# Routing the second and third sequence inside the tail of attention

## The reference

```python
x = x + L0_attn(layernorm(x))   # 16 heads of 8, causal, ALiBi bias; out @ Wo + bo
x = x + L0_ffn(layernorm(x))    # 8 experts, top 1, capacity 4096/8 = 512:
#   logits = x @ Wr + br ; gate = max(softmax) ; idx = argmax
#   pos = cumsum(one_hot(idx)) over all tokens in order ; kept where pos < capacity
#   out = gate * (relu((gate*x) @ W1[idx] + b1) @ W2[idx] + b2)
x = x + L1_attn(layernorm(x))   # attention over the 4 sequences at each position, tanh before softmax
x = x + L1_ffn(layernorm(x))    # x @ weight.T + pooled(x) @ disha
```

## Time and profile before

| | us |
|---|---|
| median of 3 runs | 681.1 (679.51 to 681.44) |
| profiled execution, its own time | 678.24 |
| its span, first to last instruction | 676.0 |
| last maximum of attention ends | 474.6 |
| first matmul of the routing stage | 505.24 |
| first load of the experts' rows | 562.12 |
| mean granted TensorE clock | 0.913 of full |

### The profile page before, as it was taken

How to read it: one execution, slowest core, us unless ns; L and a number is a source line. 1 busy time by engine, 2 the same in 40 slices (tenths; PEclk the granted TensorE clock), 3 DMA queues, 4 the chain that set the end, 5 groups by cost and what they waited for, 6 DMA issues and landing times. The chain is left out here.

```text
span 676.0 us, 13740 instructions
## 1 busy us (share of the span) xinstructions
PE 534.4 (79%) x4905; PEld 251.8 (37%) x4905; DVE 501.2 (74%) x1035; ACT 418.7 (62%) x737; POOL 234.8 (35%) x333
## 2 busy tenths in 40 slices
PE   3774798899999899998898888988867617957774
PEld 1441233333233223333333233333127615835563
DVE  4999878889888888789895988889008732626796
ACT  1971278787887787787786767867861412316651
POOL 2563012212212215222323224621621671078821
PEclk9886599999999999999999999989998757976897
DMA  7379355466533353121340120401013247310122
GB/s 181 88 175 280 99 128 119 116 149 196 145 83 68 67 114 67 39 42 31 68 89 19 41 56 28 121 20 37 10 25 114 71 136 284 111 28 21 35 48 63
DMA packets 66891, 61.11 MB, mean 90 GB/s; under 512 B 12121, under 2 KB 56058, under 8 KB 66812
## 3 DMA queue, kind: packets, MB, share of 16 engines
q1 hardware_dynamic: 58100, 53.93, 31.6%
q0 software_dynamic: 2560, 3.38, 1.7%
q10 hardware_dynamic: 6164, 2.94, 1.6%
HBM read 33.03 MB, written 29.85 MB: 93 GB/s over the span
## 5 line engine op out<-in xcount | busy, mean ns | idle before, releaser
L933 DVE TENSOR_REDUCE neg_max<-bank 128x2 f32<-128x1024 f32 (+2 forms) x320 | 341.4, 1113 | 62.8 <-PE bank L829 60.0
L973 ACT ACTIVATE probs<-ring 128x512 f32<-128x512 f32 (+4 forms) x480 | 301.8, 682 | 73.6 <-PE ring L857 62.7
L857 PE MATMUL ring<-q_operand,k_operand 56*128 56x512 bf16 (+3 forms) x768 | 161.7, 331 | 18.7 <-ACT probs L973 13.9
L878 PE MATMUL sums<-probs,v_all 128*9 128x512 f32 (+3 forms) x1536 | 161.5, 493 | 6.6 <-POOL probs L1022 4.3
L1022 POOL TENSOR_SCALAR_AFFINE_SELECT probs<-probs 128x512 f32<-128x512 f32 x128 | 80.5, 634 | 210.8 <-ACT probs L973 210.4
L829 PE MATMUL bank<-k_operand,q_operand 54*128 54x512 bf16 (+3 forms) x768 | 141.4, 340 | 9.1 <-DVE v_all L613 5.3
L857 PEld LDWEIGHTS ring<-q_operand,k_operand 56*128 56x128 bf16 x768 | 49.4, 94 | 146.0 <-ACT probs L973 103.9
L823 PE MATMUL bank<-masks 64*128 64x128 bf16 (+2 forms) x768 | 70.9, 225 | 6.8 <-DVE neg_max L933 5.8
L829 PEld LDWEIGHTS bank<-k_operand,q_operand 54*128 54x128 bf16 x768 | 46.0, 97 | 26.7 <-DVE neg_max L933 15.1
L823 PEld LDWEIGHTS bank<-masks 64*128 64x128 bf16 x768 | 36.2, 96 | 40.9 <-DVE neg_max L933 27.2
L1469 POOL DMA_INDIRECT early<-expert_out,back x32 | 32.7, 1022 | 38.3 <-issue 38.3
(11 more groups left out here) (208 smaller groups left out, 657.5 us busy)
## 6 DMA issues: line engine op xcount, KB each, us to landing
q_operand<-q_rows SPq DMA_DIRECT2D x64, 96.0 KB, 3.8
k_operand<-k_rows SPq DMA_DIRECT2D x32, 192.0 KB, 4.5
q_rows<-early SPq DMA_DIRECT2D x36, 128.0 KB, 2.4
k_rows<-early SPq DMA_DIRECT2D x36, 128.0 KB, 2.4
expert_rows<-fill SPq DMA_DIRECT2D x16, 257.0 KB, 4.2
rows<-expert_rows SPq DMA_DIRECT2D x8, 514.0 KB, 6.6
weighted_sums<-osum SPq DMA_DIRECT2D x126, 18.0 KB
sums_in<-in_L_attn_x SPq DMA_DIRECT2D x4, 512.0 KB, 7.3
```

Source lines behind the costliest of these rows:

```text
L857: last = nc.tensor.matmul(psS[:, bank, w * j:w * j + w], k_op[rows, buf, p, P * kb:P * kb + P], q_op[rows, buf, c, p, q0:q0 + w], start=Tr ...
L878: last = nc.tensor.matmul(psO[32 * i:32 * i + HD + 1, q0:q0 + w], v_all[:, n, kb, i, :], probs[:, u % NPROBS, i // 2, i % 2, 0:w], start=u ...
L933: nc.vector.tensor_reduce(neg_max[:, n % 2, slot, kc, :, pairs[0]:pairs[-1] + 1, t % CH], src, AX.X, ALU.max, negate=True).then_inc(a_read, 1)
L973: nc.scalar.activation(dst, src, ACT.Exp).then_inc(ring_read, 1)
```

## The change

The routing of the second and third sequence (chunks 2 to 5) up to their places moves from the routing stage to the tail of attention, behind the last maximum. The results of the matmuls go to the four halves of the maxima's banks. A new table `TAIL_AT` places the steps by tick (116 is unit 8 of group 14, 131 the last unit of group 15); all of TensorE's stand in the queue right behind the weighted sums of that unit. The copies of columns and the scales are VectorE's here, the power stays with GpSimd, the exponential of the logits with ScalarE. `add_bias` moves from ticks 23 and 24 to 11 and 12 for every sequence. What the routing stage keeps of sequences 1 and 2 is gating (now in steps of one chunk) and the sends.

```diff
-EARLY_AT = {6: ["reciprocals"], 7: ["store_reciprocals"], 9: ["load_reciprocals"], 20: ["divide"], 21: ["divide"],
-            23: ["bias"], 24: ["bias"]}
+EARLY_AT = {6: ["reciprocals"], 7: ["store_reciprocals"], 9: ["load_reciprocals"], 11: ["bias"], 12: ["bias"], 20: ["divide"], 21: ["divide"]}
+TAIL_AT = {116: [("project", 2)], 117: [("project", 3), ("add", 2), ("add", 3), ("moments", 2)],
+           119: [("turned", 2), ("columns", 2), ("moments", 3), ("power", 1)], 120: [("turned", 3), ("columns", 3), ("scales", 1)],
+           121: [("logits", 2)], 122: [("project", 4)], 123: [("logits", 3), ("choose", 1), ("add", 4), ("moments", 4)],
+           124: [("project", 5)], 125: [("counts", 1), ("exps", 1), ("add", 5), ("moments", 5), ("power", 2)],
+           126: [("turned", 4), ("columns", 4), ("place", 1)], 127: [("turned", 5), ("columns", 5), ("scales", 2)],
+           128: [("logits", 4)], 129: [("logits", 5), ("choose", 2)], 131: [("counts", 2), ("exps", 2), ("place", 2)]}
+TAIL_PE = {"project": 900, "turned": 700, "logits": 500, "counts": 500}
+LATE_PROJ, LATE_TURN, LATE_LG = {2: 0, 3: 1, 4: 1, 5: 3}, {2: 2, 3: 3, 4: 0, 5: 1}, {1: 0, 2: 3}
...
+            for name, c in TAIL_AT.get((n - H // GH - 1) * NU + u, []):
+                assert not a_todo
+                order.append(("E", n, "late_" + name, c // QC, c))
+                pe += TAIL_PE[name] + 2 * DRAIN if name in TAIL_PE else 0
...
+                def late_project(k):
+                    if k == QC:
+                        pe.wait_ge(a_read, NG * NM)
+                    elif k == QC + 2:
+                        pe.wait_ge(x1_ready, QC + 2)
+                    elif k == QC + 3:
+                        pe.wait_ge(late_xt, 2)
+                    pe.wait_ge(at_ready, k + 1)
+                    for i in range(CH):
+                        last = nc.tensor.matmul(half[LATE_PROJ[k]][:, P * i:P * i + P],
+                                                ot[:, k // QC, CW * (k % QC) + P * i:CW * (k % QC) + P * i + P], w["wo"][:, :],
+                                                start=True, stop=True)
+                    last.then_inc(late_proj, 1)
+                def late_turned(k):
+                    pe.wait_ge(x1_ready, k + 1)
+                    if k == QC + 2:
+                        pe.wait_ge(lg_ready, 2)
+                    for i in range(CH):
+                        last = nc.tensor.transpose(half[LATE_TURN[k]][:, P * i:P * i + P], rows[:, CH * k + i, X1:X1 + D], ident[:, :])
+                    last.then_inc(late_turn, 1)
+                def late_logits(k):
+                    pe.wait_ge(late_xt, k - QC + 1)
+                    if k == 2 * QC:
+                        pe.wait_ge(x1_ready, 3 * QC)
...
+                def late_counts(b):
+                    pe.wait_ge(hot_ready, b + 1)
+                    pe.wait_ge(late_xt, 1)
+                    pe.wait_ge(slot_ready, b)
+                    place_counts(b, half[2][:, 0:KB * E]).then_inc(late_pos, 1)
...
+                def late_add(k):
+                    dve.wait_ge(late_proj, k - QC + 1)
+                    dve.wait_ge(xb_ready, k + 1)
+                    x1 = rows[:, CH * k:CH * k + CH, X1:X1 + D]
+                    nc.vector.tensor_tensor(x1, x1, half[LATE_PROJ[k]].rearrange("p (i d) -> p i d", i=CH), ALU.add).then_inc(x1_ready, 1)
+                def late_columns(k):
+                    dve.wait_ge(late_turn, k - QC + 1)
+                    if k >= 2 * QC:
+                        dve.wait_ge(late_lg, k - 2 * QC + 1)
+                    nc.vector.tensor_copy(r["xt2"][:, k % 2, :], half[LATE_TURN[k]]).then_inc(late_xt, 1)
...
+                        elif name == "late_power":
+                            pool.wait_ge(ve2_ready, QC * (c + 1))
+                            t = slice(KB * c, KB * c + KB)
+                            nc.gpsimd.tensor_tensor(r["rs2"][:, t], r["ve2"][:, t], half_pow[:, 0:KB], ALU.pow).then_inc(pw2_ready, 1)
...
-        items["gated", r] = ("act", 3800 if r < EARLY else 1900, 0, [("place", r)])
+        for i in range(QC if r < EARLY else 1):
+            items["gated", QC * r + i] = ("act", 1900, 0, [("place", r)])
...
-            items["send", u] = ("pool", 1280, 0, [("gated", r)] if u < TILES - CH else [("gated_last", 0)])
-    for i in [(name, k) for name in ("project", "add", "moments", "turned", "columns", "logits", "take") for k in GROUPS[0]]:
+            items["send", u] = ("pool", 1280, 0, [("gated", u // CH)] if u < TILES - CH else [("gated_last", 0)])
+    for i in [(name, k) for name in ("project", "add", "moments", "turned", "columns", "logits", "take") for k in range(K0)]:
         del items[i]
-    for name in ("power", "scales", "choose", "exps", "counts", "place", "gated"):
-        del items[name, 0]
+    for i in [(name, b) for name in ("power", "scales", "choose", "exps", "counts", "place") for b in range(EARLY)] + [("gated", c) for c in range(QC)]:
+        del items[i]
...
-    K0, K1 = QC * EARLY, QC
+    K0 = K1 = QC * EARLY
```

More of the change, by code:

```diff
@@ L881, in weighted_sums @@
                     last.then_inc(pv_done, 1)
+                def late_project(k):
[22 more added lines that the diff above has]
+                        pe.wait_ge(x1_ready, 3 * QC)
+                    for i in range(CH):
+                        c0 = E * (CH * (k % QC) + i)
+                        last = nc.tensor.matmul(half[LATE_LG[k // QC]][:, c0:c0 + E], r["xt2"][:, k % 2, P * i:P * i + P], wrc[:, :],
+                                                start=True, stop=True)
+                    last.then_inc(late_lg, 1)
+                def late_counts(b):
[3 more added lines that the diff above has]
+                    place_counts(b, half[2][:, 0:KB * E]).then_inc(late_pos, 1)
                 for kind, n, *args in ORDER:
@@ L946, in _ @@
                         maxima(n, *args)
+                    elif kind == "E" and args[0] == "late_add":
+                        late_add(args[2])
+                    elif kind == "E" and args[0] == "late_moments":
+                        dve.wait_ge(x1_ready, args[2] + 1)
+                        router.moments(dve, args[2])
+                    elif kind == "E" and args[0] == "late_columns":
+                        late_columns(args[2])
+                    elif kind == "E" and args[0] == "late_scales":
+                        dve.wait_ge(pw2_ready, args[2] + 1)
+                        router.scales(dve, slice(KB * args[2], KB * args[2] + KB)).then_inc(scales_ready, 1)
+                    elif kind == "E" and args[0] == "late_choose":
+                        late_choose(args[2])
+                    elif kind == "E" and args[0] == "late_place":
+                        dve.wait_ge(late_pos, args[2])
+                        router.place(dve, args[2], half[2][:, 0:KB * E].rearrange("p (u e) -> p u e", e=E))
                     elif kind == "E" and args[0] == "reciprocals":
@@ L1669, in project @@
                 pe.wait_ge(at_ready, k + 1)
[L1670 to L1672 removed]
+            src = at[:, k - K0, :]
             for i in range(CH):
@@ L1858, in gated @@
         def gated(i):
-            act.wait_ge(slot_ready, i + 1)
-            for u in range(KB * i, min(KB * i + KB, TILES - CH)):
+            act.wait_ge(slot_ready, i // QC + 1)
+            for u in range(CH * i, CH * i + CH):
                 nc.scalar.activation(rows[:, u, XG:XG + D], rows[:, u, X1:X1 + D], ACT.Identity, bias=nt2[:, 1, u:u + 1],
```

43 lines of the change are left out of this document (30 added, 13 removed).

## The result

The changed kernel takes 670.2 us, the median of 4 runs (669.15 to 670.59), where the kernel before took 681.27 on the same chip: a ratio of 0.9859, with a 95% interval of 0.9834 to 0.9883. That is 11.1 us less. Its profiled execution took 669.15 us with a span of 667.0, 9.0 under the span of before.

What follows compares the result with a forecast made beforehand. No engine is full throughout; the tail follows the scores-exponentials-weighted sums loop, and two queues end the routing stage together. Terms 7.0 + 1.0 + 1.6 − 20.9 = −11.3 us gave 666.9 profiled, 669.8 median, said as 670, range 663 to 678.

Steps and rivals of the forecast that it cites:

- The tail, +8.0 in two terms: Tail of attention: 11.6 us of added TensorE work lengthens it by 7.0 us, powers ahead of masks by 1.0.
- The second term, +1.0 for powers ahead of masks: Tail: two GpSimd powers standing ahead of masks that weighted sums wait for cost 1.0 us, between 0 and 3.3.
- the third rival: Tail: TensorE's in-order queue stands at VectorE's late steps; slower by 13 us, 694; chance 0.07 slower, 0.04 draw.
- its sign of being wrong: Tail: TensorE waiting on VectorE for more than 3 us in all would show the prediction wrong.
- The last weighted sum near 511: End of attention: sign of the forecast; under 507 would mean better cover, over 515 the third rival's waits.
- The bias move, 0: Attention: moving the bias adds 12 weighted sums earlier changes nothing, between -0.8 and +0.8 us.
- The seam, +1.6: Last weighted sum to next block: 3.7 us in place of 2.1, as sequence 2's places come behind; between 0 and +5.
- The routing stage, −20.9: From the new block's first matmul (T) to the first load of experts' rows: 36 us against 56.9.
- the sum from the landing of the last sums to the last add: Routing stage: sums land at T+6.2, then divisions, broadcast, projection at 2.05 and add, ending about T+11.7.
- Both queues end together: Routing stage: GpSimd's sends end it at T+35.8, the sync engine's loads at T+35.9.
- the 666.9 of the sum: Whole kernel: profiled execution of 678.24 us less the summed 11.3; the runs' median, 2.9 above, gives 669.8.
- the prediction's fear of a thinner stage: Routing stage: less TensorE activity may keep the clock throttled at 1.2 GHz; projection therefore taken at 2.05 us.

Runs made afterwards that it cites:

- the doubled projections: Changed kernel with each of the four late projections in the tail computed twice into the same bank: 667.86 us, ratio 0.9841 to the kernel before.
- the bias adds alone: Kernel before with only the bias adds moved, to ticks 11 and 12 from 23 and 24: 678.93 us, ratio 0.9999.
- the fastest version: Changed kernel with stores and four sends in the tail, one send behind each of the last four masks, exponential ahead: 664.38 us, ratio 0.9772.
- powers ahead of all sends: Changed kernel with the last sequence's two powers ahead of every send in GpSimd's routing-stage order: 677.98 us, ratio 0.9983.
- four sends in the tail: Changed kernel with stores in the tail, exponential ahead, four sends moved into the tail: behind the last mask 667.73 us; behind each of the last four 664.38.
- powers later: Changed kernel with the routing stage's two powers three sends later: 673.11 us; with stores in the tail and 24 loads early too: 673.76 us.
- stores in the tail: Changed kernel with the sync engine storing the rows of chunks 0 to 5 inside the tail of attention: 668.35 us, ratio 0.9832.
- the bias adds back: Changed kernel with the bias adds back at ticks 23 and 24: 672.36 us, ratio 0.9881.
- swapped: Changed kernel with projections of chunks 6 and 7 swapped in TensorE's routing-stage order, both adds waiting for both projections: 669.52 us, ratio 0.986.
- the exponential ahead: Changed kernel with the third sequence's exponentials ahead of ScalarE's last copy and its two DMA issues: 669.26 us, ratio 0.9877.

## Why the prediction was right, and where it was not

It said 670, in a range of 663 to 678, and faster with 0.89; 670.2 was measured. It was right in its mechanism and partly by terms that cancelled.

- **The tail, +8.0 in two terms: right in size.** 7.5 was measured. TensorE took 11.1 us more (forecast 11.6) and held 0.915 of the tail (forecast 0.913). That the two shares agree so closely is luck in part: 0.913 came from a window with a granted clock of 0.94, and the same window in the trace after has 1.00 and a share of 26.75/30 = 0.89. That TensorE's work sets the tail's length is supported by the doubled projections, not proved. The second term, +1.0 for powers ahead of masks, does not show by itself: TensorE's waits on masks in the tail fell from 2.6 us in the kernel before to 1.4. In other executions of the changed kernel and its variants, where the granted clock dipped near the end of the tail, it was up to 1.7 us longer.
- **TensorE would not stand at late steps: right.** No matmul waited for VectorE in the tail, so the third rival fell. Its weight loads did for 2.8 us, just under the 3 us that the prediction named as its sign of being wrong, and hidden behind other matmuls.
- **The last weighted sum near 511: 508.5**, because the maxima ended 2.15 us earlier in this execution. That is not the edit's: the order of work up to the last maximum is the same in the changed kernel and in the run with the bias adds alone, where they ended at 475.3. What does differ in the traces is the granted clock. It was 0.89 over the first 150 us and 1.00 from 444 to 474 in the trace after, 0.87 and 0.94 in the kernel before and with the bias adds alone. In the changed kernel and its variants the first share was between 0.85 and 0.89, and the maxima ended between 471.9 and 475.5.
- **The bias move, 0: right**, 0.9999.
- **The seam, +1.6: +2.2.** The term had the exponential behind ScalarE's copy alone. It stood behind the two DMA issues as well, 0.9 us that the earlier trace rows showed. Putting it ahead of the copy and the issues took 1.5 us off the seam.
- **The routing stage, −20.9: −17.9. This is the term that was mis-sized.** The first send came at T + 1.3, not 0.8. The last add came at T + 17.0 (15.5 to 17.2 in the other runs with its order of sends), not 11.7. GpSimd's bubble at the power was 3.9 us, not 1. The step that failed is the sum from the landing of the last sums to the last add, which took each step of VectorE to follow TensorE as promptly as it does without sends. Without sends its total holds: T + 11.3 was measured. Its terms cancelled there: the sums had landed by T + 5.3 in the trace after, not T + 6.2, and the projection took 1.05, but the moments of chunk 6 stand between the two adds, 1.4 us which the sum left out. (The terms as listed give 11.45, not 11.7.) The choice of 2.05 us for the projection was not what decided: the two projections are recorded at 1.92 and 1.16 in the trace after, and the add still was 5.3 us late.
- **Both queues end together: no longer.** From the last add to the experts' load it took 22.0 us instead of 24.2; the sync queue was through at 549.39 and GpSimd's last send at 550.68. The sync queue has slack now, which is why moving its stores bought nothing that could be told.

The profiled execution took 669.15, 2.2 us above the 666.9 of the sum: +0.6 at the seam, +3.0 in the routing stage and +1.2 in the stages behind it, −0.5 in the tail and −2.1 at the maxima. The step from it to the median cancelled most of the rest: the sum added 2.9, but the median of the changed kernel stands only 1.0 above its profiled execution, 1.8 less. So the hit of 670 is luck in part: the tail was forecast well, the chain behind T was 3 us short, and two things that the change has no part in, the earlier last maximum and the place of the profiled execution among its runs, gave that back.

The clock of the routing stage was at 0.59, so it ran mostly at 1.2 GHz as forecast. The 0.60 of the earlier trace rows is that of the second part alone. Whole stage against whole stage it fell, from 0.65 to 0.59, which fits the prediction's fear of a thinner stage. But the fastest version, with the same matmuls there in 33.9 us, has 0.65 again, so what sets the share stays open.

## What to carry to other kernels

Work that fits into an idle engine's gap costs what the engine with the least room in that stretch pays for it; a first estimate of that price is the share that the same engine reaches in a fuller window next door (here within 0.5 us). When work is moved behind the last instruction of a block, list everything that stands ahead of it in each queue, DMA issues too. And where a long string of independent sends could start at once, try how many of them stand ahead of the short dependent chain which the later half of the sends needs: none or twelve in front were both slower than nine. Four of them in the gaps of the stage before, which leaves five in front, took 3.7 to 5.1 us off the routing stage (T + 33.9 for T + 37.6 and 39.0). No run has five in front with all 24 sends kept in the stage, so what the shorter string alone would give is open.

## What the runs showed of the hardware that was not expected

**VectorE's waits on TensorE grow under an unbroken string of indirect sends.** By the number of sends in the first string behind T, the last add came at:

```
sends in the string   last add at T +   clock, first 15.5 us   runs
 0                    11.3              0.72                   powers ahead of all sends
 5                    11.8, 11.9        0.83, 0.83             four sends in the tail (two runs)
 9                    15.5 to 17.2      0.72, one 0.61         the changed kernel and five variants with its order
12                    20.4, 21.1        0.50, 0.72             powers later (two runs)
```

Here the five variants are those with stores in the tail, the bias adds back, the projections twice or swapped, and the exponential ahead; the two profiles of the changed kernel itself gave 17.0 and 15.6. TensorE's clock does not explain the order of the rows: at the same 0.72 stand 11.3, 15.5 to 17.0 and 21.1. The clock's part in the 20.4 and in the step from five to nine is not separated. The copy of `back` on VectorE waits for nothing but matmuls, which are recorded as over 13 us before it, and shows the same: it starts at 553.1 in the trace after and at 547.6 in the fastest version, 2.4 and 2.3 us behind the last send, and in the run with the powers first, where the sends went on until T + 44.7, at 563.1, 3.4 us behind the last one and after 27.4 us of waiting. In the two runs with the powers later the sends paused for 3.1 us just before its matmuls ended (until 544.96 and 548.34), and there it started within 0.1 us of their recorded end. The four copies, trace after, powers first, powers later, both queues:

```profile
553.13 0.19 DVE L1682 CAST back<-ring 128x32 uint32<-128x32 f32 x1 [13.60 <-remote]
...
563.13 0.19 DVE L1685 CAST back<-ring 128x32 uint32<-128x32 f32 x1 [27.39 <-remote]
...
545.06 0.19 DVE L1685 CAST back<-ring 128x32 uint32<-128x32 f32 x1 [0.25 <-issue]
...
548.44 0.19 DVE L1699 CAST back<-ring 128x32 uint32<-128x32 f32 x1 [0.25 <-PE ring L1860]
```

 The kernel before has the late copy too, 563.6 with the last send ending at 560.9.

It is not that every such wait suffers: the places of the last sequence followed their counts within 0.6 us in the midst of the sends in the run with the stores in the tail, and VectorE's steps that wait for no matmul, such as the gating at 538.42 in the trace after, ran there without a gap. That sends cause the late starts is shown by adding and taking them away. Through what they do it, whether TensorE's results come late or VectorE starts late, is open; the recorded ends of matmuls are modelled, and no run here separates the two.

**A block's end waits for sends**, as far as one trace can show it. With GpSimd's last send ending at 513.14, the next block began 2.45 us later; VectorE's last step, which otherwise sets it, had ended at 512.37. Sends that ended 2.7 us ahead of the next block's start (509.87 and 512.61) did not hold it.

**The clock in the tail.** With TensorE at some nine tenths busy, the window from 473 to 509 us had a granted clock between 0.93 and 1.00 from execution to execution, and 1.00 in two: in the run that gave TensorE the most to do there (33.8 us of 36) and in one that gave it less (32.0). So a dip near the end of the tail is not told by the load alone; what decides it stays open.
